# Two graph convolutions in pairs of tiles: one scan and one signal for two transposes and two products

## The chip, the cores and the metric

The kernel runs on one core of a Trainium2 chip. The core has five engines that run side by side: TensorE (PE, products and transposes), VectorE (DVE), ScalarE (ACT), GpSimd (POOL) and SyncE (SP); SP and POOL issue transfers here. Time is device microseconds of one execution, from the timed runs without the profiler; the lower the better. Engines hand work to each other by semaphores.

## The reference, cut to what matters

The model has two layers on a graph of 50000 nodes with 128 features and 25000 edges, sorted by their target. The first is an attention layer over typed edges (not touched here). The second does two graph convolutions in a row over the same edges:

```python
def _graph_conv(h, src, dst, W, b):
    n = h.shape[0]
    ones = jnp.ones(src.shape[0], dtype=h.dtype)
    out_deg = jnp.clip(jax.ops.segment_sum(ones, src, num_segments=n), 1.0)
    in_deg = jnp.clip(jax.ops.segment_sum(ones, dst, num_segments=n), 1.0)
    h = h * jax.lax.rsqrt(out_deg)[:, None]
    agg = jax.ops.segment_sum(h[src], dst, num_segments=n)
    agg = agg * jax.lax.rsqrt(in_deg)[:, None]
    return jax.nn.relu(agg @ W + b)

h = _graph_conv(features, src, dst, W1, b1)
h = _graph_conv(h, src, dst, W2, b2)
...
x = x + _L1_gnn_ref(h, ...)
```

## The kernel before, in words

The edges are cut into `ET` = 196 tiles of 128. Both convolutions are one function, `conv_phase(second)`, called twice; each walks over the 196 tiles, and each engine has its own list of instructions, written out in full.

For tile n, with edges on partitions and features in columns:

- POOL gathers the 128 source rows from memory into `row` (L1592). A ring of `R` = 14 tiles holds them; gather n waits for transpose n-14.
- In the second convolution ACT multiplies the rows by the source's factor (L1629), in place.
- PE transposes the tile into `pT` (L1644), so that edges lie along the columns.
- DVE scans along the edges (L1669): state = keep x state + value. `keep` is 0 where a new target begins and 1 elsewhere, so the state at a target's last edge is the sum over its edges. The scan starts with the last column of the tile before, so the scans form one chain through all 196 tiles. The result goes to the ring `sT`.
- PE multiplies by the weights (L1650) into `pm`; the scan's result is the stationary operand. An fp32 product is two instructions in the profile, a transpose one.
- DVE scales by the target's factor and adds the bias (L1676).
- First convolution: ACT applies the ReLU (L1632) and SP stores the tile to the table `t1` (L1619), from which the second one gathers. Second convolution: DVE applies the ReLU and adds the old x in one operation (L1681), for which SP loads the tile `rx` (L1615), and POOL scatters the rows to the output (L1598), only those of a target's last edge.

What sets the order: PE does transpose n, then product n-1; `pT` and `pm` have two buffers each, so transpose n waits for scan n-2 and product n-1 waits for the evacuation n-3. DVE does scan n, then evacuation n-2 (and, in the second, its residual). POOL does, in the second convolution, gather n, then scatter n-8 (`LAG` = 8). SP loads a piece of `keep` of 14 tiles (448 KB) at n = 0, 14, 28, ... in the first convolution, in the same queue as the stores, which stand at n-8; the second uses the same `keep`. Between the two convolutions all engines meet at a barrier, and the stores of `t1` have landed.

## Time and profile before

| | |
|---|---|
| time, 3 runs | median 3132.02 us (3129.52 to 3133.0) |
| the profiled execution | 3122.26 us, of which the span 3120.6 us |
| first convolution, first gather to the barrier | 2257 to 2555 us |
| second convolution, first gather to last scatter | 2555 to 3113 us |
| TensorE's granted clock over the span | 0.769 |

The profile is of one execution. A row of the timeline gives an instruction's start and length in microseconds, and in brackets how long its engine had been idle and what it waited for. What is named as the releaser is inferred from semaphores, and can be the name of a transfer of another stage that once used the same semaphore. For PE, the start and length are those of the issue, with a modelled end: when its result was really there shows only in who waits for it. "issue" means that the profile shows nothing that was waited for.

### The profile page before, as it was taken

To read this page: it belongs to the slowest core of one execution; us is meant where nothing else is said; L and a number is where in the kernel's file an instruction comes from. 1 tells how busy PE (TensorE), PEld (TensorE's weight loads), DVE (VectorE), ACT (ScalarE), POOL (GpSimd) and SP (SyncE) were. 2 spreads that over 40 slices of the span, in tenths; PEclk is the share of its full clock that TensorE was granted. 3 is DMA by queue.
4 is the path that set the end of the run, shared out by engine and by line. 5 is a ranking of instruction groups with operands and counts; after the bars stand their busy time and mean duration, and the time that the engine had idled before them with its cause. 6 is when DMAs were issued, how large, how long until landed. Compare 5 with 4: busy or idle time off the path is not lost. (4 is left out here: it accounts for less than half of the span.)

```text
span 3120.6 us, 48869 instructions
## 1 busy us (share of the span) xinstructions
PE 1916.5 (61%) x12706; PEld 1487.4 (48%) x12706; DVE 2069.9 (66%) x6764; ACT 1160.4 (37%) x3211; POOL 1837.1 (59%) x2417
## 2 busy tenths in 40 slices
PE   4620006889888889898886378778555553333333
PEld 1100005788888888888886245444334432222222
DVE  7975546888888788788786777777634443333333
ACT  0000005666666666666663245545412221111111
POOL 0003327777777777777774245454466657666766
PEclk9965557999999999999998689898755555555555
DMA  1016755666666666666663244444334442222221
GB/s 48 0 37 232 246 184 146 155 157 155 156 157 155 157 152 157 158 156 151 157 157 93 52 128 116 127 122 121 98 101 116 115 101 65 64 67 63 64 64 49
DMA packets 400270, 374.38 MB, mean 120 GB/s; under 512 B 60254, under 2 KB 342269, under 8 KB 397032
## 3 DMA queue, kind: packets, MB, share of 16 engines
q1 hardware_dynamic: 360856, 276.76, 33.2%
q0 software_dynamic: 31360, 64.76, 10.0%
q10 hardware_dynamic: 7806, 29.98, 2.4%
q8 instruction: 104, 1.70, 0.2%
q14 instruction: 144, 1.18, 0.1%
HBM read 227.43 MB, written 147.13 MB: 120 GB/s over the span
## 5 line engine op out<-in xcount | busy, mean ns | idle before, releaser
L814 POOL DMA_INDIRECT att_xsd<-xt,ends_i x392 | 405.0, 1033 | 179.7 <-issue 136.6
L1669 DVE TENSOR_TENSOR_SCAN conv_sT<-keep,conv_sT,conv_pT 128x128 f32<-128x128 bf16 x390 | 186.5, 478 | 485.3 <-DMA t<-conv_res 193.7
L1650 PE MATMUL conv_pm<-w,conv_sT 128*128 128x128 f32 x784 | 280.1, 460 | 358.6 <-DVE conv_res L1676 226.9
L1650 PEld LDWEIGHTS conv_pm<-w,conv_sT 128*128 128x128 f32 x784 | 196.9, 311 | 450.0 <-issue 321.2
L1008 PE MATMUL att_kvc<-att_hm,w_kv 128*128 128x128 f32 x2352 | 296.3, 276 | 0.0
L1118 DVE TENSOR_TENSOR att_kvm<-att_kvc,att_rel_in 128x1024 f32<-128x1024 f32 x196 | 239.0, 1219 | 62.5 <-PE att_kvc L1021 50.3
L1008 PEld LDWEIGHTS att_kvc<-att_hm,w_kv 128*128 128x128 f32 x2352 | 280.3, 193 | 0.0
L1354 POOL TENSOR_TENSOR edge_glm<-edge_gl,edge_mask 128x1536 f32<-128x1536 f32 (+1 forms) x56 | 153.2, 2736 | 211.9 <-PE edge_pc L1445 205.1
L952 ACT ACTIVATE att_nhb<-att_nxr 128x128 f32<-128x128 f32 x391 | 168.7, 478 | 277.3 <-DMA att_nxr<-xt 276.9
L1107 DVE TENSOR_TENSOR att_hm<-att_hT,att_mask_in_t 128x768 f32<-128x768 f32 x196 | 186.3, 951 | 114.9 <-issue 106.3
L1598 POOL DMA_INDIRECT out_dram<-conv_res,out_i x196 | 198.1, 1011 | 108.6 <-issue 101.3
L1644 PE MATMUL conv_pT<-ident,conv_row 128*128 128x128 f32 x392 | 168.7, 430 | 147.7 <-issue 117.0
L1629 ACT ACTIVATE conv_row<-conv_row,ats 128x128 f32<-128x128 f32 x196 | 78.7, 401 | 474.1 <-DMA conv_row<-t,idx 454.9
L1592 POOL DMA_INDIRECT conv_row<-ta,idx x196 | 185.5, 946 | 103.5 <-issue 40.9
L1592 POOL DMA_INDIRECT conv_row<-t,idx x196 | 191.9, 979 | 77.2 <-issue 56.1
L1021 PE MATMUL att_kvc<-tab,att_noh 9*128 9x128 bf16 x391 | 53.6, 217 | 280.7 <-DMA att_noh<-node_hot 277.4
L1059 PE MATMUL att_msgp<-att_kvm,rel_v 128*128 128x128 f32 x1568 | 224.1, 290 | 0.0
L1057 PE MATMUL att_keyp<-att_kvm,rel_k 128*128 128x128 f32 x1568 | 223.2, 289 | 0.5 <-DVE att_prod L1099 0.5
L1059 PEld LDWEIGHTS att_msgp<-att_kvm,rel_v 128*128 128x128 f32 x1568 | 208.6, 207 | 0.0
L1057 PEld LDWEIGHTS att_keyp<-att_kvm,rel_k 128*128 128x128 f32 x1568 | 205.0, 204 | 5.0 <-issue 0.7
L1076 DVE BATCH_NORM_STATS2 att_nst<-att_nx 128x6 f32<-128x128 f32 x782 | 190.3, 285 | 13.5
L931 ACT ACTIVATE msg_all<-att_msgp 128x128 f32<-128x128 f32 x196 | 54.4, 278 | 324.4 <-PE att_msgp L1059 315.6
(242 smaller groups left out, 5012.0 us busy)
## 6 DMA issues: line engine op xcount, KB each, us to landing
att_mask_in_t<-type_row SPq DMA_DIRECT2D x196, 192.0 KB
xt<-xr ACTq DMA_DIRECT2D x23, 1224.0 KB
att_nxr<-xt SPq DMA_DIRECT2D x97, 262.0 KB
att_rel_in<-rel_row SPq DMA_DIRECT2D x196, 128.0 KB
out_dram<-att_not SPq DMA_DIRECT2D x97, 256.0 KB
ta<-att_nhs SPq DMA_DIRECT2D x97, 256.0 KB
xr<-in_x_dram SPq DMA_DIRECT2D x22, 1088.0 KB
xd_rows<-att_xsd SPq DMA_DIRECT2D x196, 65.5 KB
```

Source lines behind the costliest of these rows:

```text
L814: pool.indirect_dma_start(out=xsd[:, v, k, :], out_offset=None, in_=xt, in_offset=bass.IndirectOffsetOnAxis(ap=ends_i[:, n, k:k + 1], axis ...
L952: m = nc.scalar.activation(nhb[:, u % 2, i], nxr[g % RN][:, j, 0:D], ACT.Relu, bias=nxr[g % RN][:, j, C_NA:C_NA + 1], scale=nxr[g % RN][:, ...
L1008: nc.tensor.matmul(kvc[:, e], w_kv[:, t, e], hm[:, w, 0, t], start=e == 0 and t == 0, stop=False)
L1057: nc.tensor.matmul(keyp[:, 0], rel_k[:, r], kvm[:, w, 0, r], start=r == 0, stop=r == RELS - 1)
L1059: m = nc.tensor.matmul(msgp[:, 0], rel_v[:, r], kvm[:, w, 1, r], start=r == 0, stop=r == RELS - 1)
L1076: m = dve.bn_stats(nst[:, k, i], of[:, u % 2 * 2 + i])
L1107: dve.tensor_tensor(hm[:, w], hT[:, 0:2].rearrange("p e (o d) -> p e o d", o=1).to_broadcast([P, 2, TYPES, P]), mask_in_t[:, k % RM], ALU. ...
L1118: dve.tensor_tensor(kvm[:, w], kvc[:, 0:2].rearrange("p a (o e) -> p a o e", o=1).to_broadcast([P, 2, RELS, P]), rel_in[:, v].rearrange("p ...
L1592: pool.indirect_dma_start(out=row[:, n % R, :], out_offset=None, in_=table, in_offset=bass.IndirectOffsetOnAxis(ap=idx[:, int(second), n:n ...
L1598: pool.indirect_dma_start(out=out, out_offset=bass.IndirectOffsetOnAxis(ap=out_i[:, k:k + 1], axis=0), in_=res[:, k % R, :], in_offset=Non ...
L1650: nc.tensor.matmul(pm[:, k % 2, 0:D], sT[:, k % R], w[:], start=True, stop=True).then_inc(m_ready, 1)
L1669: dve.tensor_tensor_scan(sT[:, n % R], keep[:, n * P:(n + 1) * P], pT[:, n % 2, 0:P], before, ALU.mult, ALU.add).then_inc(s_ready, 1)
```

## The change

The two convolutions work on pairs of tiles, `H` = 98 passes. The rings hold `RP` = 14 pairs instead of 14 tiles, so twice the rows. PE transposes both tiles of pair p into one buffer of `pT`, with one signal, and then does both products of pair p - `AHEAD` = p-3, with one signal. `pT` and `pm` have four buffers each. DVE scans both tiles in one instruction of 256 columns, then evacuates the two products of pair p-4 in two instructions, and in the second convolution adds the residual in one of 256 columns. ACT applies the ReLU to a pair at once; its scaling in the second convolution stays one instruction a tile, with one signal for the pair. SP stores and loads pairs; the piece of `keep` for seven pairs is loaded at p = 0, 7, 14, ..., ahead of the store of pair p-4. POOL's gathers and scatters stay one a tile; `LAG` is 16 tiles, and waits are one a pair.

```diff
@@ -1545,8 +1545,12 @@
-        R = 14
-        CHUNKS = ET // R
+        H = ET // 2
+        RP = 14
+        USES = H // RP
+        KP = 7
+        NBANK = 4
+        AHEAD = 3
         keep = sb("keep", [P, EP], BF16)
         idx = sb("idx", [P, 2, ET], I32)

@@ -1564,21 +1568,21 @@

     ls, clear = phase_sems(name + "_")

-    LAG = 8
+    LAG = 16
     table, w, b_all = (t1, w_2, b2_all) if second else (ta, w_1, b1_all)
-    row = lb("row", [P, R, D], F32)
-    sT = lb("sT", [P, R, P], F32)
-    res = lb("res", [P, R, D], F32)
-    rx = lb("rx", [P, R, D], F32) if second else None
-    pT = lp("pT", [P, 2, 512], F32)
-    pm = lp("pm", [P, 2, 512], F32)
+    row = lb("row", [P, RP, 2, D], F32)
+    sT = lb("sT", [P, RP, 2 * P], F32)
+    res = lb("res", [P, RP, 2, D], F32)
+    rx = lb("rx", [P, RP, 2, D], F32) if second else None
+    pT = lp("pT", [P, NBANK, 512], F32)
+    pm = lp("pm", [P, NBANK, 4, D], F32)
...
     with nc.Block() as block:
         @block.gpsimd
@@ -1587,98 +1591,111 @@
                 pool.wait_ge(idx_ready, 2)
             for n in range(ET + (LAG if second else 0)):
                 if n < ET:
-                    if n >= R:
-                        pool.wait_ge(t_ready, n - R + 1)
-                    pool.indirect_dma_start(out=row[:, n % R, :], out_offset=None, in_=table,
+                    p = n // 2
+                    if p >= RP and n % 2 == 0:
+                        pool.wait_ge(t_ready, p - RP + 1)
+                    pool.indirect_dma_start(out=row[:, p % RP, n % 2, :], out_offset=None, in_=table,
                                             in_offset=bass.IndirectOffsetOnAxis(ap=idx[:, int(second), n:n + 1], axis=0)
-                                            ).then_inc(got[n % R], 16)
+                                            ).then_inc(got[p % RP], 16)
                 k = n - LAG
                 if second and k >= 0:
-                    pool.wait_ge(res_ready, k + 1)
+                    q = k // 2
+                    if k % 2 == 0:
+                        pool.wait_ge(res_ready, q + 1)
                     pool.indirect_dma_start(out=out, out_offset=bass.IndirectOffsetOnAxis(ap=out_i[:, k:k + 1], axis=0),
-                                            in_=res[:, k % R, :], in_offset=None, bounds_check=N - 1,
-                                            oob_is_err=False).then_inc(stored[k % R], 16)
+                                            in_=res[:, q % RP, k % 2, :], in_offset=None, bounds_check=N - 1,
+                                            oob_is_err=False).then_inc(stored[q % RP], 16)
...
         @block.sync
         def _(sp):
-            for n in range(ET + LAG):
-                if n < ET and n % R == 0 and not second:
-                    c = n // R
-                    sp.dma_start(keep[:, c * R * P:(c + 1) * R * P],
-                                 keep_row[c * R * P:(c + 1) * R * P].partition_broadcast(P)).then_inc(keep_in[c], 16)
-                k = n - LAG
-                if k >= 0 and not second:
-                    sp.wait_ge(res_ready, k + 1)
-                    sp.dma_start(t1[k * P:(k + 1) * P], res[:, k % R]).then_inc(stored[k % R], 16)
+            for p in range(H + AHEAD + 1):
+                if p < H and p % KP == 0 and not second:
+                    c, w0 = p // KP, KP * 2 * P
+                    sp.dma_start(keep[:, c * w0:(c + 1) * w0],
+                                 keep_row[c * w0:(c + 1) * w0].partition_broadcast(P)).then_inc(keep_in[c], 16)
...
+                q = p - AHEAD - 1
+                if q >= 0 and not second:
+                    sp.wait_ge(res_ready, q + 1)
+                    sp.dma_start(t1[q * 2 * P:(q + 1) * 2 * P].rearrange("(j e) d -> e j d", e=P), res[:, q % RP]).then_inc(stored[q % RP], 16)
...
         @block.scalar
...
         @block.tensor
         def _(pe):
-            for n in range(ET + 1):
-                if n < ET:
+            for p in range(H + AHEAD):
+                if p < H:
                     if second:
-                        pe.wait_ge(scaled, n + 1)
+                        pe.wait_ge(scaled, p + 1)
                     else:
-                        pe.wait_ge(got[n % R], n // R * 16 + 16)
-                    if n >= 2:
-                        pe.wait_ge(s_ready, n - 1)
-                    nc.tensor.transpose(pT[:, n % 2, 0:P], row[:, n % R], ident[:]).then_inc(t_ready, 1)
-                k = n - 1
-                if k >= 0:
-                    pe.wait_ge(s_ready, k + 1)
-                    if k >= 2:
-                        pe.wait_ge(v_ready, k - 1)
-                    nc.tensor.matmul(pm[:, k % 2, 0:D], sT[:, k % R], w[:], start=True, stop=True).then_inc(m_ready, 1)
+                        pe.wait_ge(got[p % RP], p // RP * 32 + 32)
+                    if p >= NBANK:
+                        pe.wait_ge(s_ready, p - NBANK + 1)
+                    for j in range(2):
+                        m = nc.tensor.transpose(pT[:, p % NBANK, j * P:(j + 1) * P], row[:, p % RP, j], ident[:])
+                    m.then_inc(t_ready, 1)
+                q = p - AHEAD
+                if q >= 0:
+                    pe.wait_ge(s_ready, q + 1)
+                    if q >= NBANK:
+                        pe.wait_ge(v_ready, q - NBANK + 1)
+                    for j in range(2):
+                        m = nc.tensor.matmul(pm[:, q % NBANK, j], sT[:, q % RP, j * P:(j + 1) * P], w[:], start=True, stop=True)
+                    m.then_inc(m_ready, 1)

         @block.vector
         def _(dve):
             if not second:
                 dve.tensor_scalar(idx[:, 0], ats[:, :, 0, 2], float(EP + NP), None, ALU.min).then_inc(idx_ready, 1)
                 dve.tensor_scalar(idx[:, 1], ats[:, :, 0, 2], float(EP), None, ALU.min).then_inc(idx_ready, 1)
-            for n in range(ET + 2):
-                if n < ET:
-                    dve.wait_ge(t_ready, n + 1)
-                    if not second and n % R == 0:
-                        dve.wait_ge(keep_in[n // R], 16)
-                    if n >= R:
-                        dve.wait_ge(m_ready, n - R + 1)
-                    if n == 0:
-                        before = 0.0
+            for p in range(H + AHEAD + 1):
+                if p < H:
+                    dve.wait_ge(t_ready, p + 1)
+                    if not second and p % KP == 0:
+                        dve.wait_ge(keep_in[p // KP], 16)
+                    if p >= RP:
+                        dve.wait_ge(m_ready, p - RP + 1)
+                    if p == 0:
+                        prior = 0.0
                     else:
-                        dve.wait_ge(s_ready, n)
-                        before = sT[:, (n - 1) % R, P - 1:P]
-                    dve.tensor_tensor_scan(sT[:, n % R], keep[:, n * P:(n + 1) * P], pT[:, n % 2, 0:P], before,
+                        dve.wait_ge(s_ready, p)
+                        prior = sT[:, (p - 1) % RP, 2 * P - 1:2 * P]
+                    dve.tensor_tensor_scan(sT[:, p % RP], keep[:, p * 2 * P:(p + 1) * 2 * P], pT[:, p % NBANK, 0:2 * P], prior,
                                            ALU.mult, ALU.add).then_inc(s_ready, 1)
-                k = n - 2
-                if k >= 0:
-                    dve.wait_ge(m_ready, k + 1)
-                    if k >= R:
-                        dve.wait_ge(stored[k % R], k // R * 16)
-                    dve.scalar_tensor_tensor(res[:, k % R], pm[:, k % 2, 0:D], ats[:, k:k + 1, 1, 1], b_all[:],
-                                             ALU.mult, ALU.add).then_inc(v_ready, 1)
+                q = p - AHEAD - 1
+                if q >= 0:
+                    dve.wait_ge(m_ready, q + 1)
+                    if q >= RP:
+                        dve.wait_ge(stored[q % RP], q // RP * (32 if second else 16))
+                    for j in range(2):
+                        k = 2 * q + j
+                        m = dve.scalar_tensor_tensor(res[:, q % RP, j], pm[:, q % NBANK, j], ats[:, k:k + 1, 1, 1], b_all[:],
+                                                     ALU.mult, ALU.add)
+                    m.then_inc(v_ready, 1)
                     if second:
-                        dve.wait_ge(x_in[k % R], k // R * 16 + 16)
-                        dve.wait_ge(v_ready, k + 1)
-                        dve.scalar_tensor_tensor(res[:, k % R], res[:, k % R], 0.0, rx[:, k % R], ALU.max,
+                        dve.wait_ge(x_in[q % RP], q // RP * 16 + 16)
+                        dve.wait_ge(v_ready, q + 1)
+                        dve.scalar_tensor_tensor(res[:, q % RP], res[:, q % RP], 0.0, rx[:, q % RP], ALU.max,
                                                  ALU.add).then_inc(res_ready, 1)
     clear()
 
```

How the lists of instructions stand now. PE at the start of the first convolution, before (`conv_pT` is the transpose, `conv_pm` the product):

```order
L1644 MATMUL conv_pT<-ident,conv_row 128x128 x2
L1650 MATMUL conv_pm<-w,conv_sT 128x128
L1644 MATMUL conv_pT<-ident,conv_row 128x128
L1650 MATMUL conv_pm<-w,conv_sT 128x128
L1644 MATMUL conv_pT<-ident,conv_row 128x128
```

and after:

```order
L1655 MATMUL conv_pT<-ident,conv_row 128x128 x8
L1663 MATMUL conv_pm<-w,conv_sT 128x128 x2
L1655 MATMUL conv_pT<-ident,conv_row 128x128 x2
L1663 MATMUL conv_pm<-w,conv_sT 128x128 x2
L1655 MATMUL conv_pT<-ident,conv_row 128x128 x2
```

Eight transposes stand before the first product, where there were two, and from then on two of each alternate.

DVE at the start of the second convolution (`conv_sT` is the scan, `conv_res` the evacuation and the residual), before:

```order
L1669 SCALAR_TENSOR_TENSOR conv_sT<-keep,conv_pT 128x128
L1669 SCALAR_TENSOR_TENSOR conv_sT<-keep,conv_sT,conv_pT 128x128 x2
L1676 SCALAR_TENSOR_TENSOR conv_res<-conv_pm,ats,b_all 128x128
L1681 SCALAR_TENSOR_TENSOR conv_res<-conv_res,conv_rx 128x128
L1669 SCALAR_TENSOR_TENSOR conv_sT<-keep,conv_sT,conv_pT 128x128
```

and after:

```order
L1683 SCALAR_TENSOR_TENSOR conv_sT<-keep,conv_pT 128x256
L1683 SCALAR_TENSOR_TENSOR conv_sT<-keep,conv_sT,conv_pT 128x256 x4
L1692 SCALAR_TENSOR_TENSOR conv_res<-conv_pm,ats,b_all 128x128 x2
L1698 SCALAR_TENSOR_TENSOR conv_res<-conv_res,conv_rx 128x256
L1683 SCALAR_TENSOR_TENSOR conv_sT<-keep,conv_sT,conv_pT 128x256
```

The first result stands behind five scans of two tiles, where it stood behind three of one tile.

SP in the first convolution (the loads of `keep` and the stores), before:

```order
L1610 DMA keep<-keep_row 128x1792
L1619 DMA t<-conv_res 128x128 x6
L1610 DMA keep<-keep_row 128x1792
L1619 DMA t<-conv_res 128x128 x14
L1610 DMA keep<-keep_row 128x1792
```

and after:

```order
L1617 DMA keep<-keep_row 128x1792
L1626 DMA t<-conv_res 128x2x128 x3
L1617 DMA keep<-keep_row 128x1792
L1626 DMA t<-conv_res 128x2x128 x7
L1617 DMA keep<-keep_row 128x1792
```

The second piece, for tiles 14 and on, stood behind the store of tile 5; now it stands behind the store of pair 2, that is of tiles 4 and 5. What differs is when that store's result is made: tile 5 by DVE's pass 7, pair 2 by its pass 6, the last one before the scan of pair 7, which is tiles 14 and 15.

## Rows read from the trace of the kernel before

**Rows 1.** Stretches, both convolutions: length, busy us (instructions) of each engine, clock, DMA share, GB/s

```profile
2257.00:2555.00 298.00, 165.51 (x588) 116.97 (x588) 136.90 (x393) 60.67 (x196) 185.46 (x196) 0.52 0.40 108
2555.00:3113.00 558.00, 191.65 (x588) 120.91 (x588) 193.35 (x588) 78.66 (x196) 389.64 (x392) 0.50 0.27 65
```

**Rows 2.** Groups by line, GpSimd: count | busy us, mean ns | idle us before

```profile
L1592 POOL DMA_INDIRECT conv_row<-ta,idx x196 | 185.5, 946 | 103.5 <-issue 40.9 <-PE conv_pT L1644 35.2 <-DMA att_noh<-node_hot 18.7
L1598 POOL DMA_INDIRECT out_dram<-conv_res,out_i x196 | 198.1, 1011 | 108.6 <-issue 101.3 <-DVE conv_res L1681 7.3
L1592 POOL DMA_INDIRECT conv_row<-t,idx x196 | 191.9, 979 | 77.2 <-issue 56.1 <-POOLq L109 17.8 <-DVE conv_res L1681 1.8
```

**Rows 3.** Timeline, ends of both stages: start, length, engine, line, operation [idle before]

```profile
2257.37 1.09 POOL L1592 DMA_INDIRECT conv_row<-ta,idx  x1 [8.73 <-DVE idx L1656]
2260.25 0.48 PE L1644 MATMUL conv_pT<-ident,conv_row 128*128 128x128 f32 x1 [17.32 <-DMA conv_row<-ta,idx]
2536.65 0.94 POOL L1592 DMA_INDIRECT conv_row<-ta,idx  x1 [0.30 <-issue]
2555.36 0.94 POOL L1592 DMA_INDIRECT conv_row<-t,idx  x1 [17.76 <-POOLq L109]
```

**Rows 4.** Timeline, VectorE: first and last scan of the first convolution

```profile
2260.76 0.42 DVE L1669 TENSOR_TENSOR_SCAN conv_sT<-keep,conv_pT 128x128 f32<-128x128 bf16 x1 [3.68 <-PE conv_pT L1644]
2549.10 0.48 DVE L1669 TENSOR_TENSOR_SCAN conv_sT<-keep,conv_sT,conv_pT 128x128 f32<-128x128 bf16 x1
```

**Rows 5.** Timeline, first convolution, where tiles go quickly

```profile
2503.12 0.48 DVE L1669 TENSOR_TENSOR_SCAN conv_sT<-keep,conv_sT,conv_pT 128x128 f32<-128x128 bf16 x1 [0.54 <-PE conv_pT L1644]
2503.76 0.48 DVE L1669 TENSOR_TENSOR_SCAN conv_sT<-keep,conv_sT,conv_pT 128x128 f32<-128x128 bf16 x1
2504.55 0.42 PE L1644 MATMUL conv_pT<-ident,conv_row 128*128 128x128 f32 x1
2505.01 0.48 DVE L1669 TENSOR_TENSOR_SCAN conv_sT<-keep,conv_sT,conv_pT 128x128 f32<-128x128 bf16 x1 [0.53 <-issue]
2505.19 0.42 PE L1644 MATMUL conv_pT<-ident,conv_row 128*128 128x128 f32 x1
```

**Rows 6.** Groups by line, VectorE: a scan of 384 columns, stage before

```profile
L1489 DVE TENSOR_TENSOR_SCAN msg_all<-edge_dB,msg_all 128x384 f32<-128x384 f32 x28 | 28.5, 1017 | 26.0 <-PE edge_dB L1429 26.0
```

**Rows 7.** Timeline, first convolution, where scans come late

```profile
2270.17 0.48 PE L1644 MATMUL conv_pT<-ident,conv_row 128*128 128x128 f32 x1 [0.34 <-DMA conv_row<-ta,idx]
2271.62 0.47 PE L1644 MATMUL conv_pT<-ident,conv_row 128*128 128x128 f32 x1
2274.09 0.48 DVE L1669 TENSOR_TENSOR_SCAN conv_sT<-keep,conv_sT,conv_pT 128x128 f32<-128x128 bf16 x1 [3.53 <-DMA att_noh<-node_hot]
2278.32 0.48 DVE L1669 TENSOR_TENSOR_SCAN conv_sT<-keep,conv_sT,conv_pT 128x128 f32<-128x128 bf16 x1 [3.50 <-DMA att_noh<-node_hot]
2293.72 0.48 DVE L1669 TENSOR_TENSOR_SCAN conv_sT<-keep,conv_sT,conv_pT 128x128 f32<-128x128 bf16 x1 [3.48 <-DMA att_noh<-node_hot]
```

**Rows 8.** Timeline of SyncE's queue, a load of `keep`; then stretches behind it

```profile
2303.35 0.43 SPq L1610 DMA_DIRECT2D keep<-keep_row  x1
...
2307.40:2308.40 1.00, 0.00 (x0) 0.00 (x0) 0.00 (x0) 0.00 (x0) 0.00 (x0) 0.50 0.48 129
2308.40:2309.40 1.00, 0.00 (x0) 0.00 (x0) 0.09 (x1) 0.00 (x0) 0.00 (x0) 0.50 0.03 8
```

**Rows 9.** Timeline, second convolution: a gather, its result, its scatter

```profile
2889.29 0.98 POOL L1592 DMA_INDIRECT conv_row<-t,idx  x1 [0.30 <-issue]
2899.50 0.29 DVE L1681 SCALAR_TENSOR_TENSOR conv_res<-conv_res,conv_rx 128x128 f32<-128x128 f32 x1
2911.37 1.01 POOL L1598 DMA_INDIRECT out_dram<-conv_res,out_i  x1 [0.30 <-issue]
```

**Rows 10.** Timeline, GpSimd, second convolution: first and last scatter that waited

```profile
2580.56 1.01 POOL L1598 DMA_INDIRECT out_dram<-conv_res,out_i  x1 [1.26 <-issue]
3094.22 1.01 POOL L1598 DMA_INDIRECT out_dram<-conv_res,out_i  x1 [2.65 <-issue]
```

37 lines of the change are left out of this document (20 added, 17 removed).

## The prediction

> **What bounds the kernel now.** I read the busy time by stage first. The change touches two stages alone: the first convolution, about 2257 to 2555 us, and the second, 2555 to 3113 us. In both TensorE's granted clock is about 0.50, the lower of its two levels, and no engine's busy time fills the stage [rows 1]. What lies ahead of 2257 us is left as it is.
>
> Then the groups by line. In the second convolution GpSimd issues 196 gathers and 196 scatters: 191.9 + 198.1 us busy, and before them 77.2 + 108.6 us idle, of which 17.8 us are the change of stage. GpSimd's own pace is one issue after another with 0.30 us between them [rows 9], so its floor is 191.9 + 198.1 + 391 x 0.30 = 507.3 us, and it took 390.0 + 168.0 = 558.0 us [rows 2]: 50.7 us above its floor. In the first convolution it issues gathers alone: floor 185.5 + 196 x 0.30 = 244.3 us, taken from 2257.37 to 2537.6, which is 280 us; the next stage's first gather starts at 2555.36 [rows 2, 3]. So the first convolution is not bound by GpSimd: the rows are there, and TensorE and VectorE are late. Their scans run from 2260.76 to 2549.10 us, 288.3 us for 195 steps, 1.479 us a tile [rows 4].
>
> Then the timeline, for what a tile costs TensorE and VectorE. There are two regimes. In the quick one, two tiles take 2503.12 to 2505.01 = 1.89 us, 0.945 a tile, though the engines alone could do better: two scans with the other VectorE operation between them lie 0.64 us apart, and two transposes with a product between them also 0.64 us (2504.55 to 2505.19) [rows 5]. The 0.3 us more is the round trip: a product waits for the scan just before it, and that scan for a transpose that stands behind the product before. In the slow one, a transpose starts at 2270.17 and the scan that reads it only at 2274.09; the next at 2271.62, its scan at 2278.32 [rows 7]. VectorE had nothing else to do; the name behind its idle time is a DMA of another stage, which it does not wait for. So what is late is TensorE's completion, by 3 to 6 us. Four steps on, a scan starts at 2293.72: 19.6 us from the first, 4.9 a tile. I don't know what causes it. What I can count is its cost: 288 us less 195 x 0.945 = 184 us is 104 us in the first convolution, 7.4 us for 14 tiles.
>
> **The change, part by part.**
>
> *Signals and order.* TensorE does two transposes, then the two products of the pair three back; nothing in a pass waits for a scan of the same pass. The round trip goes, and what is late next is TensorE itself at 0.64 us a tile, 1.28 a pair. VectorE: a 128-wide scan and one evacuation cost 0.64; a scan of 256 columns I put between the 0.48 of 128 and the 1.017 of 384 columns [rows 5, 6], 0.75 us, so a pair is 0.64 + 0.27 + 0.33 = 1.24 us, no more than TensorE. Bounds: the scan costs 0.48 at the least and 1.02 at the most, the pair 0.97 to 1.51. In the second convolution the residual over 256 columns adds at most 2 x 0.29, and GpSimd takes 5.2 us a pair, so nothing of this shows there.
>
> *The slow regime* is left: the number of transposes and products is the same. I keep 7.4 us for 14 tiles. It could go down to 0, if fewer waits of TensorE make it rarer, or stay in full.
>
> *The table `keep`.* This edit speaks against the change. SyncE loads a piece of 448 KB every 14 tiles and stands in its own queue behind the store of a result. Before, the store ahead of it is that of tile n-9, and the load has some seven tiles of time. After, it is the store of pair p-5, whose result VectorE makes in the last pass before the one that needs the piece. So each of 13 loads is waited for: the ReLU, 0.4 us, the issue of the store and the load, 0.7 us, and the transfer. Traffic after the load issued at 2303.35 dies away by 2308.4 [rows 8], with other traffic in it; the smallest transfer shown, a gather to its transpose, takes 2257.37 to 2260.25 = 2.9 us [rows 3]. Between 2.9 and 5.0 I take 4.0, nearer the load's own row; the wait is 5.1 us. Behind it on VectorE stand all later scans and evacuations. TensorE has three pairs in hand, 3 x 1.28 = 3.8 us, so it loses 5.1 - 3.8 + the scan's 0.75 = 2.0 us every 14 tiles.
>
> *First convolution, the sum.* Per 14 tiles: 14 x 0.64 = 9.0, slow regime 7.4, `keep` 2.0, together 18.4 us, against GpSimd's 14 x 1.25 = 17.5. So TensorE's side still sets it, by a little: 14 x 18.4 = 258 us from a first scan at 2260.8 + 1.25 (a pair needs two gathers), that is to 2520; before, 6.3 us lie between the last scan's start and the next stage's first gather, and I add 0.5 for the longer tail: 2526 against 2555.4, a gain of 29 us. The best is GpSimd's floor: last gather 2257.4 + 195 x 1.25 = 2501.1, + 2.9 to its transpose, + 0.6 to the scan, + 6.8 = 2511.4, a gain of 44. The worst, with nothing hidden, is in the rivals.
>
> *Second convolution, the sum.* GpSimd waits only where a result is late for its scatter. Before, the gather at 2889.29 has its result at 2899.79, and its scatter starts at 2911.37: 11.6 us of reserve [rows 9]. The scatters that wait longer than 0.4 us are 27, in 13 clusters, the first at 2580.56 and the last at 3094.22 [rows 10]; these are the slow regime, when results slip past the reserve. After, a scatter stands 16 gathers back instead of 8, at 16 x 2.60 + 1.3 = 42.9 us behind its gather. But its result waits for the scan of four pairs on, nine gathers later: 9 x 2.60 = 23.4, then the 5.3 us that also remain before (10.5 less two periods), and 1.35 for a second scaling (0.40), transpose (0.21), the wider scan (0.27), a second evacuation (0.33) and the wider residual (0.14): 30.0. Reserve 12.9, or 1.3 us more for 13 clusters: 17 us. Doubling the distance buys so little because the deeper pipeline spends it. I take 22, near that end; the bounds are 0 and the whole 50.
>
> *Everything else*: half as many stores, of 128 KB, off the path; one ReLU instead of two, hidden behind GpSimd's 1.25 us a tile; start and end of the second stage keep their single gathers and scatters. Nothing.
>
> *A rule that could speak against it.* In the second convolution TensorE now works in bursts, one in 5.2 us instead of 2.6, and the clock there is already at its lower level, 0.50 [rows 1]. The Trainium skill, "TensorE: Matmul & The Clock Gate", section "Loop structure matters more than you think", says that waits between bursts of products send the engine back to its cold clock. By the trace this costs 0, since there is nothing to lose; by the rule, had the stage run at 2.4 GHz, a tile's 0.64 would have been half and would now double, still under the 2.60 of GpSimd.
>
> Total: 29 + 22 = 51 us. The profiled execution took 3122.3 us, so 3071; the median of the runs shown is 3132.0, 9.8 above it, and I carry that over: 3081 us.
>
> **Rivals.**
>
> B, the late completions lose their bite: with three pairs of slack both stages run at GpSimd's floor. 44 + 50 us: 3122.3 - 94 + 9.8 = 3038. For it: the slow regime is a matter of lateness, and slack absorbs lateness. Against it: in it TensorE serves a tile in 4.9 us and one arrives in 1.25, and slack does not add service.
>
> C, the load of `keep` is paid in full in the first convolution, because it and the slow regime fall apart in time and the three pairs in hand are mostly done when the wait starts. Per 14 tiles 9.0 + 7.4 + 5.1 = 21.5 us, 301 in all against 288: 13 us lost, 22 won in the second: 3123.
>
> D, slower: C, and the round trip does not go, because the wide scan sits at its upper bound and every pair is handed on in lumps. Then 14 x 0.945 + 7.4 + 5.1 = 25.7 us, 360 in all: 72 lost, 22 won, 3182. It decides as soon as 14 tiles of the first convolution cost more than 20.7 + 22/14 = 22.3 us. For it: both new dependences sit in that stage. Against it: nothing in a pass waits for the same pass any more.
>
> E: the change does not reach the path, the slow regime fills whatever is freed: 3132.
>
> **How the numbers follow.** My forecast 0.56, B 0.17, C 0.14, D 0.08, E 0.05. The predicted time is 3081. The range runs to the times of B and C, 3040 to 3125, and leaves out about 0.2. A measurement of this kernel tells 0.2%, 6 us, from no change. Faster: forecast, B and half of C (which ends 9 us below the median, at the edge of what counts), 0.80; same: E and 0.03 of C, 0.08; slower: D and the last 0.04 of C, 0.12.
>
> **What would show it.** Right: between slow stretches transposes of a pair and products of a pair follow each other at 1.28 us a pair or at GpSimd's 2.5; scans of 256 columns near 0.75 us; every seventh scan of the first convolution waits 3 to 5 us behind the load of `keep`; the next stage's first gather near 2526; in the second convolution fewer scatters wait, and the slow stretches are still there. Wrong: slow stretches gone or shorter (B), 14 tiles of the first convolution above 20.7 us (C, D), scans above 1 us, or a second convolution still 50 us above GpSimd's floor.

## The result, and the profile after

The changed kernel takes 3154.05 us (median of 4 runs, 3152.42 to 3156.05) against 3132.51 for the kernel before beside it (4 runs, 3129.52 to 3136.21): ratio 1.0069, 95% interval 1.0058 to 1.0081. It is slower by 21.5 us; I had forecast 51 us faster, and the time lies outside my range.

The two convolutions in the view of stretches, from each one's first gather (columns as in [rows 1], which these answer to; the second reaches to the end of the execution here):

```profile
2258.95:2572.85 313.90, 125.19 (x588) 109.38 (x588) 117.23 (x294) 40.84 (x98) 185.06 (x197) 0.60 0.37 103
2572.85:3153.10 580.25, 153.47 (x588) 120.27 (x588) 162.11 (x392) 67.90 (x196) 390.16 (x392) 0.51 0.26 62
```

The work got cheaper as planned: VectorE's busy time in the first falls from 136.9 to 117.2 us. The stage got longer all the same, 313.9 us for 298.0, although TensorE's granted clock rose in it from 0.52 to 0.60. The groups by line say that the instructions cost what I took, and that GpSimd waits more for results (busy, mean ns | idle before, releasers; the GpSimd rows answer to [rows 2]):

```profile
L1683 DVE TENSOR_TENSOR_SCAN conv_sT<-keep,conv_sT,conv_pT 128x256 f32<-128x256 bf16 x194 | 144.2, 744 | 562.4 <-DMA t<-conv_res 213.7 <-PE conv_pT L1655 167.5 <-issue 90.9
L1605 POOL DMA_INDIRECT out_dram<-conv_res,out_i x196 | 197.9, 1010 | 120.0 <-issue 66.3 <-DVE conv_res L1698 53.7
L1597 POOL DMA_INDIRECT conv_row<-t,idx x196 | 192.3, 981 | 91.6 <-issue 58.5 <-POOLq L109 32.3 <-DMA t<-conv_res 0.9
```

A scan of 256 columns takes 744 ns. The scatters' idle time is 120.0 us, before 108.6; the gathers' is the same once the wait between the stages is taken off (91.6 - 32.3 against 77.2 - 17.8).

The ends of the stages on the timeline, as in [rows 3]:

```profile
2258.95 1.09 POOL L1597 DMA_INDIRECT conv_row<-ta,idx  x1 [8.73 <-DVE idx L1670]
2539.63 0.94 POOL L1597 DMA_INDIRECT conv_row<-ta,idx  x1 [0.30 <-issue]
2572.85 0.94 POOL L1597 DMA_INDIRECT conv_row<-t,idx  x1 [32.27 <-POOLq L109]
3141.35 0.98 POOL L1605 DMA_INDIRECT out_dram<-conv_res,out_i  x1 [0.30 <-issue]
```

The two profiled executions (spans 3153.1 and 3120.6) lie 32.5 us apart, and the medians only 21.5: the profiled one of the kernel before is 10 us quicker than its median. The parts below are those of this one pair, so the sizes of the middle two are uncertain by some 10 us. The 32.5 us divide into:

| part | us |
|---|---|
| first convolution starts later | 1.6 |
| its first gather to the next stage's: 313.9 for 298.0 | 15.9 |
| GpSimd waits longer for results in the second | 11.4 |
| last scatter's start to the end: 11.8 for 8.2 | 3.6 |

A second profiled execution of the changed kernel (after_again, below) has 310.0 us in the first convolution and 571.1 from there to the end, where the kernel before has 298.0 and 565.2: 12.0 and 5.9 us lost, 3.6 of the latter at the end. That the second convolution won nothing is thus seen twice; the 11.4 us is not (2.3 there).

The 15.9 us divide again, by the times of the scans. The first 13 pairs take 68.2 us where the first 26 tiles took 51.1: 17.1 lost. The rest takes 233.0 where it took 237.3: 4.2 won. The first scan comes 1.25 us later behind the first gather, and the stage ends 1.8 us later behind the last scan. So most of the loss is one place, the first stretch of late completions:

```profile
2276.49 0.75 DVE L1683 TENSOR_TENSOR_SCAN conv_sT<-keep,conv_sT,conv_pT 128x256 f32<-128x256 bf16 x1 [1.57 <-issue]
2289.88 0.75 DVE L1683 TENSOR_TENSOR_SCAN conv_sT<-keep,conv_sT,conv_pT 128x256 f32<-128x256 bf16 x1 [12.14 <-DMA att_noh<-node_hot]
2306.06 0.75 DVE L1683 TENSOR_TENSOR_SCAN conv_sT<-keep,conv_sT,conv_pT 128x256 f32<-128x256 bf16 x1 [14.94 <-DMA att_noh<-node_hot]
2319.36 0.75 DVE L1683 TENSOR_TENSOR_SCAN conv_sT<-keep,conv_sT,conv_pT 128x256 f32<-128x256 bf16 x1 [12.05 <-DMA att_noh<-node_hot]
```

The scans come 13.4, 16.2 and 13.3 us apart. The releaser named, a DMA of an earlier stage, is only the nearest event of the record; in the trace's semaphore events each of the last three scans starts 0.03 us behind TensorE's signal that the pair is transposed (2289.85, 2306.03, 2319.33), and that signal is what is late. This is the slow regime of [rows 7]; in the kernel before a tile took up to 6.3 us there, and a pair takes up to 16.2 now.

After that the stage goes in cycles of seven pairs, most of them 20 to 21 us long and 19.4 on average (233.0 us for 84 pairs). The last gap of a cycle is the wait for `keep`:

```profile
2436.46 0.75 DVE L1683 TENSOR_TENSOR_SCAN conv_sT<-keep,conv_sT,conv_pT 128x256 f32<-128x256 bf16 x1 [5.16 <-DMA att_noh<-node_hot]
...
2438.59 0.47 SPq L1617 DMA_DIRECT2D keep<-keep_row  x1
2438.63 0.44 PEld L1655 LDWEIGHTS conv_pT<-ident,conv_row 128*128 128x128 f32 x2
2438.84 0.64 PE L1655 MATMUL conv_pT<-ident,conv_row 128*128 128x128 f32 x2
...
2443.53 0.75 DVE L1683 TENSOR_TENSOR_SCAN conv_sT<-keep,conv_sT,conv_pT 128x256 f32<-128x256 bf16 x1 [5.83 <-issue]
...
2444.90 0.93 PEld L1663 LDWEIGHTS conv_pm<-w,conv_sT 128*128 128x128 f32 x4 [5.83 <-issue]
2444.93 1.19 PE L1663 MATMUL conv_pm<-w,conv_sT 128*128 128x128 f32 x4 [5.46 <-DVE conv_res L1692]
```

The load is issued behind the result of the pair before it, 2.1 us after that pair's scan, and the scan starts 4.9 us later, 7.1 us behind the one before instead of 1.2. Over the twelve loads behind the first stretch the gap is 4.8 to 5.9 us longer than 1.2, on average 5.4. TensorE's last transposes end at 2439.5; then it idles for over 5 us.

### The profile page after: what moved, and what is told of

Same layout as the page of the kernel before. It is cut to its first block and busy times, and to the rows that moved or that the text cites. A ratio compares the mean times of both kernels' runs of the same rounds, so it can differ in the third digit from the quotient of the medians.

```text
span 3153.1 us, 47390 instructions
## 1 busy us (share of the span) xinstructions
PE 1835.9 (58%) x12706; PEld 1475.2 (47%) x12706; DVE 2020.3 (64%) x6470; ACT 1129.0 (36%) x3113; POOL 1836.0 (58%) x2417
## 5 line engine op out<-in xcount | busy, mean ns | idle before, releaser
L1683 DVE TENSOR_TENSOR_SCAN conv_sT<-keep,conv_sT,conv_pT 128x256 f32<-128x256 bf16 x194 | 144.2, 744 | 562.4 <-DMA t<-conv_res 213.7
L1655 PE MATMUL conv_pT<-ident,conv_row 128*128 128x128 f32 x392 | 122.2, 412 | 401.8 <-issue 249.2
L1663 PE MATMUL conv_pm<-w,conv_sT 128*128 128x128 f32 x784 | 201.2, 408 | 199.1 <-DVE conv_res L1692 128.0
L1663 PEld LDWEIGHTS conv_pm<-w,conv_sT 128*128 128x128 f32 x784 | 176.7, 311 | 216.3 <-DVE conv_sT L1683 111.6
L1655 PEld LDWEIGHTS conv_pT<-ident,conv_row 128*128 128x128 f32 x392 | 65.3, 204 | 433.9 <-issue 270.0
L1597 POOL DMA_INDIRECT conv_row<-t,idx x196 | 192.3, 981 | 91.6 <-issue 58.5
L1638 ACT ACTIVATE conv_row<-conv_row,ats 128x128 f32<-128x128 f32 x196 | 67.9, 393 | 483.7 <-DMA conv_row<-t,idx 467.0
```

The source lines that it names most:

```text
L1597: pool.indirect_dma_start(out=row[:, p % RP, n % 2, :], out_offset=None, in_=table, in_offset=bass.IndirectOffsetOnAxis(ap=idx[:, int(seco ...
L1655: m = nc.tensor.transpose(pT[:, p % NBANK, j * P:(j + 1) * P], row[:, p % RP, j], ident[:])
L1663: m = nc.tensor.matmul(pm[:, q % NBANK, j], sT[:, q % RP, j * P:(j + 1) * P], w[:], start=True, stop=True)
```

## Experiments

My theory after the result: two steps of the sum failed, the wait for `keep` (5.4 us for 2.0 in a cycle) and the reserve of the second convolution. The rival: the late completions have no fixed price, and take back whatever slack is given.

The runs fell on four chips, and these differ. The kernel before takes 3124.4 and 3131.5 us in two sessions on one of them, like the 3132.5 of the first result (its chip isn't known), and 3027.6, 3028.0 and 3027.1 on the three others. Nearly all of the 100 us lies in the two convolutions: b_lag12, on one of the three, has 254.5 and 515.1 us there against 298.0 and 565.2, 93.6 of the 96.7 us between the two spans, and its trace shows no late stretch of TensorE's signals. Ratios are to the kernel before on the same chip and in the same session; I call these *late* and *punctual* chips, though only the late one was used in more than one session.

The late traces differ in one more way. They lack records of semaphore events, of all engines, and most where the completions are late. In the first convolution of the kernel before, 279 of TensorE's 392 signals are recorded and 97 signals of VectorE's 196 scans; in b_lag12 on the punctual chip, nearly all. The same kernel compared stage by stage:

| stretch | semaphore events, b_lag12_2 (late) | b_lag12 (punctual) | TensorE's signals in the late one |
|---|---|---|---|
| 1000 to 1300 us | 5647 | 7080 | up to 1.3 us late |
| 2000 to 2240 us | 1820 | 1780 | in time |
| 2600 to 3000 us, second convolution | 1225 | 8177 | many us late |

The traces hold equally many instructions, 48869. So the recording of events and the late signals go together, and a rival is that the recording itself holds TensorE up on that chip. No run settles it: the times are said above to be those of runs without the profiler, but every timed run of the experiments has a span and a granted clock on record, so none is known to have run with nothing recording.

| run | edit | chip | us | ratio, 95% interval |
|---|---|---|---|---|
| a_keep | `keep` 7 pairs earlier | punctual | 3033.3 | 1.0020, 1.0011 to 1.0030 |
| a_keep_lag24 | + scatters 24 tiles behind | punctual | 3033.4 | 1.0017, 1.0008 to 1.0027 |
| b_lag12 | before, scatters 12 behind | punctual | 3028.0 | 1.0005, 0.9996 to 1.0015 |
| b_fill | before, wide filler | punctual | 3027.4 | 1.0001, 0.9991 to 1.0010 |
| after_again | the changed kernel | late | 3141.2 | 1.0054, 1.0038 to 1.0071 |
| a_keep_2 | as a_keep | late | 3134.1 | 1.0029, 1.0016 to 1.0041 |
| a_keep_lag24_2 | as a_keep_lag24 | late | 3128.4 | 1.0013, 1.0003 to 1.0022 |
| b_lag12_2 | as b_lag12 | late | 3124.7 | 0.9999, 0.9989 to 1.0008 |
| b_fill_2 | as b_fill | late | 3155.5 | 1.0069, 1.0053 to 1.0086 |
| b_fill_tiny | before, narrow filler | late | 3152.7 | 1.0068, 1.0051 to 1.0085 |
| b_onepass | before, one product pass (weights left out) | late | 3115.2 | 0.9942, 0.9925 to 0.9958 |
| a_keep_fill | a_keep + wide filler, 3 buffers for 4 | late | 3165.9 | 1.0109, 1.0092 to 1.0126 |
| b_allbf16 | before, all bf16 | punctual | 3027.3 | 1.0000, 0.9990 to 1.0010 |
| a_allbf16 | a_keep, all bf16 | punctual | 3030.4 | 1.0010, 1.0000 to 1.0019 |
| b_plain | before, plain row loads (permutation left out) | punctual | 2979.7 | 0.9845, 0.9829 to 0.9862 |
| b_bf16w | before, products bf16 | punctual | 3026.5 | 0.9998, 0.9989 to 1.0008 |
| b_allbf16_2 | as b_allbf16 | punctual | 3026.7 | 0.9998, 0.9989 to 1.0008 |
| b_plain_2 | as b_plain | punctual | 2979.8 | 0.9845, 0.9829 to 0.9862 |

### The wait for keep: a_keep, after_again, a_keep_2

```diff
-if p < H and p % KP == 0 and not second:
-    c, w0 = p // KP, KP * 2 * P
-    sp.dma_start(keep[...piece c...])
+if p < H and p % KP == 0 and not second:
+    for c in ((0, 1) if p == 0 else (p // KP + 1,)):
+        if c < H // KP: sp.dma_start(keep[...piece c...])
```

> The changed kernel, with each piece of keep loaded seven pairs earlier (two pieces at the start). Theory 1, the load of keep is waited for in full: the changed kernel's first convolution goes in a fixed cycle of 20.3 us for 14 tiles, of which 5.6 us are the late piece. Without it 14.7 us are left, under GpSimd's 17.5, so the stage falls to about 260 us from 313 and the kernel to about 3100, 0.990 of before. Rival, the slow regime sets the cycle and only fills other waits: the stage stays at 300 us or more and the kernel at 3140 or more.

> The changed kernel itself, beside the kernel before. Two cases. If the kernel before takes about 3132 us here (late TensorE completions present): this one 3154 again, the first gather of the second convolution 314 us after that of the first, seven scans per 20.3 us. If the kernel before takes about 3028 us (none present): my theory says that the late load of keep costs nothing at all there, since seven pairs take TensorE and VectorE 6 x 1.28 + 6.8 = 14.5 us and GpSimd's gathers of them 14 x 1.249 = 17.5 us: the gathers stay 1.25 us apart, and the time is that of the version with keep loaded seven pairs earlier, 3033 (ratio 1.002), 3.6 us of which are GpSimd's drain at the end of the second convolution (7.6 us instead of 4.0). Rival: the wait for keep is paid there too, 13 x 5 = 65 us, 3095.

> The changed kernel with each piece of keep loaded seven pairs earlier (two at the start). With late completions present: my theory is that 5.6 of the 20.3 us of seven pairs in the first convolution are the wait for keep. Without it the seven take 14.7 us and GpSimd's own 17.5 us bound them: 13 x 2.8 = 36 us less than the changed kernel, 3118, with the second convolution unchanged (568 us). Rival (the late completions follow the scans whatever these wait for, the wait only covers them): 20 us per seven pairs stay, 3154. Without late completions: 3033, as before.

On the late chip the early load gives 7 us, where my theory said 36 and the rival none. The wait is gone, some 65 us in twelve loads, and the first convolution falls only from 310.0 us in after_again to 301.4: the late completions fill most of the place. The scans of a_keep_2 in one cycle, with the same columns as above:

```profile
2437.45 0.75 DVE L1685 TENSOR_TENSOR_SCAN conv_sT<-keep,conv_sT,conv_pT 128x256 f32<-128x256 bf16 x1 [6.45 <-DMA att_noh<-node_hot]
2438.62 0.74 DVE L1685 TENSOR_TENSOR_SCAN conv_sT<-keep,conv_sT,conv_pT 128x256 f32<-128x256 bf16 x1
...
2443.23 0.74 DVE L1685 TENSOR_TENSOR_SCAN conv_sT<-keep,conv_sT,conv_pT 128x256 f32<-128x256 bf16 x1
2444.81 0.75 DVE L1685 TENSOR_TENSOR_SCAN conv_sT<-keep,conv_sT,conv_pT 128x256 f32<-128x256 bf16 x1 [0.34 <-PE conv_pT L1657]
2453.24 0.75 DVE L1685 TENSOR_TENSOR_SCAN conv_sT<-keep,conv_sT,conv_pT 128x256 f32<-128x256 bf16 x1 [7.18 <-DMA att_noh<-node_hot]
2460.24 0.75 DVE L1685 TENSOR_TENSOR_SCAN conv_sT<-keep,conv_sT,conv_pT 128x256 f32<-128x256 bf16 x1 [5.76 <-DMA att_noh<-node_hot]
```

More pairs go quickly now (1.2 us apart), but the two late ones come 8.4 and 7.0 us apart; this cycle, 2437.45 to 2460.24, holds eight pairs in 22.8 us. Over everything behind the first 13 pairs a tile takes 1.34 us here (224.5 us for 84 pairs), 1.39 in the changed kernel (233.0) and 1.40 in the one before (237.3 us for 169 tiles). On the punctual chip the gathers of a_keep stand 1.25 us apart throughout and no slack is needed; what is left of the change costs 6 us, 3.6 of them the end of the last stage. No run shows the late load of `keep` on a punctual chip.

Both convolutions on the punctual chip, first of b_lag12 (near enough the kernel before) and then of a_keep:

```profile
2254.27:2508.78 254.51, 176.79 (x588) 122.46 (x588) 138.56 (x392) 60.60 (x196) 185.07 (x197) 0.50 0.46 127
2508.78:3023.90 515.12, 178.05 (x588) 119.85 (x588) 198.72 (x588) 78.65 (x196) 388.86 (x392) 0.50 0.30 70
```

```profile
2252.94:2509.02 256.08, 141.77 (x588) 117.43 (x588) 122.35 (x294) 40.79 (x98) 185.08 (x197) 0.55 0.46 126
2509.02:3028.90 519.88, 149.65 (x588) 121.08 (x588) 164.05 (x392) 67.91 (x196) 389.99 (x392) 0.50 0.30 69
```

In both kernels both stages stand at GpSimd's floor (244 and 507 us by the prediction's sums from [rows 2], plus filling and draining). The change saves TensorE, VectorE and ScalarE 28, 35 and 11 us of work in the second convolution, and none of it is on the path.

### More reserve: b_lag12, b_lag12_2, a_keep_lag24, a_keep_lag24_2

```diff
-                LAG = 8
+                LAG = 12
```

(in the changed kernel with the early load, 16 becomes 24)

> The kernel before, with the scatter 12 gathers behind instead of 8 and nothing else. Reserve 11.6 + 10.4 = 22 us against a delay of 15: theory 1 says that nearly no scatter waits, the second stage falls from 557 to 508 us and the kernel to about 3083, 0.984. Rival (something else holds GpSimd): 3132.

> The kernel before with each scatter of the second convolution 12 tiles behind its gather instead of 8. With late completions present: the reserve grows from 11.6 to 16.8 us, over the 15.4 us that the tiles fall behind in a stretch, so the 13 clusters of stalls of 4 us go: 3132 - 50 = 3082. Rival (average pace, not reserve, is the bound): 3125 or more. Without late completions: 3028, no change.

> As a_keep, and the scatter of the second convolution stands 24 gathers behind instead of 16. Theory 1 for the second stage, the deeper pipeline used up the reserve (13 us, while a slow stretch delays a result by 19): with 34 us of reserve no scatter waits, the stage falls from 568 us to GpSimd's 507, and the kernel to about 3040, 0.970 of before. Rival, GpSimd is held by something else than late results: the second stage stays above 550, the kernel near 3100.

> The same, and in the second convolution each scatter follows its gather by 24 tiles instead of 16. With late completions present: GpSimd's reserve grows from 13 to some 23 us (8 x 1.3 more), over the 18.8 us by which the pairs fall behind in a stretch; the some 12 stalls of 5.5 us go: 3118 - 60 = 3058. Rival (the pairs fall behind by whatever the reserve allows, since TensorE and VectorE are slower on average than GpSimd): under 20 us gained, 3100 or more. Without late completions: 3033.

My reserve theory falls: 4 tiles more give nothing (0.9999), 8 more give 5.7 us where it said 60. The room given is larger than the expectations of b_lag12_2 and a_keep_lag24_2 say: a tile of distance is a gather and a scatter, 2.6 us and not 1.3. Where nothing is late, a scatter starts 11.6 us behind its result in the kernel before [rows 9] and 22.0 us (median) in b_lag12, 13.2 us in a_keep and 34.0 in a_keep_lag24. So 10 us more of room bought nothing, and 21 us more bought 5.7. The pace over many tiles is what binds, and lateness grows into the room it gets. Scans of b_lag12_2 in the second convolution, the last quick one and those behind it:

```profile
2830.70 0.47 DVE L1669 TENSOR_TENSOR_SCAN conv_sT<-keep,conv_sT,conv_pT 128x128 f32<-128x128 bf16 x1
2834.24 0.48 DVE L1669 TENSOR_TENSOR_SCAN conv_sT<-keep,conv_sT,conv_pT 128x128 f32<-128x128 bf16 x1 [2.42 <-DMA t<-conv_res]
2839.16 0.48 DVE L1669 TENSOR_TENSOR_SCAN conv_sT<-keep,conv_sT,conv_pT 128x128 f32<-128x128 bf16 x1 [3.80 <-DMA t<-conv_res]
...
2853.89 0.48 DVE L1669 TENSOR_TENSOR_SCAN conv_sT<-keep,conv_sT,conv_pT 128x128 f32<-128x128 bf16 x1 [4.50 <-DMA t<-conv_res]
2860.90 0.48 DVE L1669 TENSOR_TENSOR_SCAN conv_sT<-keep,conv_sT,conv_pT 128x128 f32<-128x128 bf16 x1 [5.89 <-DMA t<-conv_res]
2867.23 0.48 DVE L1669 TENSOR_TENSOR_SCAN conv_sT<-keep,conv_sT,conv_pT 128x128 f32<-128x128 bf16 x1 [5.20 <-DMA t<-conv_res]
2868.27 0.47 DVE L1669 TENSOR_TENSOR_SCAN conv_sT<-keep,conv_sT,conv_pT 128x128 f32<-128x128 bf16 x1
```

The gaps grow from 3.5 to 7.0 us and then drop to 1.04. Late stretches (over 2 us in which a TensorE signal comes over 0.15 us behind its instruction's end, from those semaphore events that are recorded) hold some 60% of the second convolution in the kernel before and some 80% here and in a_keep_lag24_2.

### Work or instructions: b_fill, b_fill_2, b_fill_tiny, a_keep_fill

```diff
 nc.tensor.matmul(pm[:, k % 2, 0:D], sT[:, k % R], w[:], ...).then_inc(m_ready, 1)
+for _ in range(3 if second else 1):
+    nc.tensor.matmul(spare[:], identb[:], keep[:, 0:512], start=True, stop=True)   # tiny: 0:8
```

(TensorE also waits for the first piece of `keep` before it starts; a_keep_fill has two and six fillers a pair, and three buffers of `pT` and `pm` instead of four)

> The kernel before, where TensorE does products that nobody reads behind each product: one of 512 columns a tile in the first convolution, three in the second, in bf16. Theory A, the late completions come with a TensorE that is mostly idle (in the attention stage, where it is busy, they are short): they vanish or shrink, scans wait less in both stages, and the kernel goes to 3040 to 3100. Theory B, they come with the number of its instructions or with time: more instructions make them as frequent or more so, 3132 to 3250.

> The kernel before with filler on TensorE in both convolutions: after each tile one (first) or three (second) bf16 products of 512 columns into a bank that nobody reads. It computes the same. Where late TensorE completions are present (the kernel before at 3124 to 3132): if a TensorE with long idle gaps delivers its completions late, the filler closes the gaps and the stretches vanish as they do in the attention stage: first convolution 254 us, second 515, some 3028 in all (ratio 0.969). If instead each TensorE instruction's completion costs time (a limit on completions), 2 more instructions beside the present 6 per tile in the first and 6 more in the second make it slower: 3200 or more. If neither: 3125. Where they are absent (3028): 3028 again.

> The same instructions, each filler product only 8 columns wide: as many TensorE instructions as in the wide filler, hardly any work. Late completions present: idle theory 3110 to 3130 (gaps stay), limit on completions 3200 or more. Absent: 3028.

> The changed kernel with keep loaded seven pairs earlier, three banks in place of four, and per pair two (first convolution) or six (second) filler products of 512 columns. Late completions present: idle theory, no stretches are left and GpSimd's floor bounds both convolutions: 3033 (ratio 0.97), no better than the same filler in the kernel before, since both stand at GpSimd's floor and this one has 3.6 us more drain at the end. Limit on completions: 3200 or more. Absent: 3033.

On the late chip both fillers cost, and as much whether wide or narrow: 24.0 and 21.2 us. More work on TensorE does not make the late stretches go. That its idle gaps cause them is not refuted by this, because the filler stands behind the product, which itself waits for a scan, so the long gaps stay. Two transposes of b_fill_2 and the products behind them:

```profile
2704.02 0.42 PE L1647 MATMUL conv_pT<-ident,conv_row 128*128 128x128 f32 x1
2708.57 0.77 PE L1653 MATMUL conv_pm<-w,conv_sT 128*128 128x128 f32 x2 [4.12 <-DVE conv_sT L1674]
...
2710.41 0.42 PE L1647 MATMUL conv_pT<-ident,conv_row 128*128 128x128 f32 x1 [0.22 <-issue]
2715.71 0.77 PE L1653 MATMUL conv_pm<-w,conv_sT 128*128 128x128 f32 x2 [4.88 <-DVE conv_res L1681]
```

In the second convolution TensorE idles for over 2 us at a time for 238 us in all with the wide filler, and for 202 us in the kernel before. Idle gaps alone are not enough, though: on the punctual chips TensorE has as little to do and nothing is late. First convolution of b_fill_2, then of b_fill_tiny:

```profile
2253.87:2557.92 304.05, 187.31 (x769) 120.30 (x785) 138.18 (x392) 60.59 (x196) 185.06 (x197) 0.75 0.39 106
```

```profile
2256.35:2562.96 306.61, 186.00 (x785) 142.48 (x785) 139.43 (x392) 60.69 (x196) 185.51 (x196) 0.50 0.38 106
```

The granted clock is 0.75 in the one and 0.50 in the other, the stages 304 and 307 us: the clock does not matter here. On the punctual chip the same wide filler is free (1.0001), so it is not its own time that costs on the late one. The limit on completions has the right sign; its 3200 or more was far too high.

### Fewer or cheaper passes: b_onepass, b_bf16w, b_allbf16, b_allbf16_2, a_allbf16

```diff
-sT = lb("sT", [P, R, P], F32)
+sT = lb("sT", [P, R, P], BF16)
-nc.tensor.matmul(pm[:, k % 2, 0:D], sT[:, k % R], w[:], ...)
+nc.tensor.matmul(pm[:, k % 2, 0:D], sT[:, k % R], identb[:], ...)   # b_bf16w: weights cast to bf16
```

(b_allbf16: the transposes too, as bf16 products of the upper halves of the fp32 words)

> The kernel before with the scans of the convolutions written in bf16 and multiplied by the bf16 identity in place of the weights: one product pass per tile instead of two, so 4 TensorE instructions per tile instead of 6 (the convolutions' weights are left out of the result). Late completions present: with a limit on completions, a tile in a late stretch takes 7.0 x 4/6 = 4.7 us, the lateness stays within the reserve of 11.6 us, and the time falls to some 3050; idle theory: 3125 or more. Absent: 3028.

> The kernel before with only the products in bf16 (scans written in bf16, weights cast), transposes in fp32. Late completions present: as with one product pass, 3115 (0.994) by the instruction theory; fp32 theory: two of three passes are gone, below 3080. Absent: 3028.

> The kernel before with both TensorE steps of the convolutions in bf16: rows go in as the upper halves of their fp32 words, the scans are written in bf16 and the weights are cast (the result is that of bf16 inputs). As many instructions per tile as with one product pass (4). Late completions present: if they belong to fp32 passes, none are left and the time is 3028; if to instructions of any kind, it is that of one product pass, 3115 (ratio 0.994). Absent: 3028.

> The same for the changed kernel with keep loaded seven pairs earlier: 8 TensorE instructions per pair instead of 12. Late completions present: fp32 theory 3033; instruction theory 16 to 20 us under its own 3134, some 3116. Absent: 3033.

> Both TensorE steps of the convolutions of the kernel before in bf16, 4 instructions per tile instead of 6. Late completions present (the kernel before at 3124 to 3132): fp32 theory, none are left, 3028 (ratio 0.967); instruction theory, 3115 (0.994). Absent: as before, 3028 and ratio 1.000.

The fp32 product is two weight loads and two products in the trace, the bf16 one is one of each. Without the second pass the time is 3115.2 us, 16.3 less than before: the sign of the instruction theory, at a fifth of the size it said (some 3050). The stretches stay, with smaller gaps. From b_onepass, second convolution:

```profile
2639.76 0.48 DVE L1669 TENSOR_TENSOR_SCAN conv_sT<-keep,conv_sT,conv_pT 128x128 bf16<-128x128 bf16 x1 [3.79 <-DMA t<-conv_res]
2645.37 0.48 DVE L1669 TENSOR_TENSOR_SCAN conv_sT<-keep,conv_sT,conv_pT 128x128 bf16<-128x128 bf16 x1 [4.48 <-DMA t<-conv_res]
2650.96 0.48 DVE L1669 TENSOR_TENSOR_SCAN conv_sT<-keep,conv_sT,conv_pT 128x128 bf16<-128x128 bf16 x1 [4.44 <-DMA t<-conv_res]
```

5.6 us is the largest steady gap here with 4 TensorE instructions (weight loads and products) per tile, 7.7 in the kernel before with 6, and 16.1 to 16.8 for a pair with 12. All are close to multiples of 0.70 us: 8, 11, 23 and 24. In the timed runs 784 instructions fewer (2 for each of 392 tiles) gave 16.3 us and some 1570 more (2 and 6 a tile) cost 24.0 and 21.2: 21, 15 and 14 ns each. The four bf16 runs all fell on punctual chips, where there is nothing to see, so the fp32 theory was not tested by them. The late traces themselves speak against it, and against a limit on instructions alone. The stage just before the convolutions, in the kernel before (columns as in [rows 1]), and its largest group:

```profile
2000.00:2240.00 240.00, 185.22 (x946) 112.52 (x944) 186.19 (x627) 121.23 (x316) 117.00 (x57) 0.90 0.43 118
```

```profile
L1445 PE MATMUL edge_pc<-w_a,edge_glm 128*128 128x128 f32 x588 | 73.8, 282 | 0.0
```

It has 588 fp32 products of the same shape and 3.9 products a us in all, where the first convolution has 2.0; all its 108 signals are recorded, each within 0.02 us. What differs is the number of signals, 0.45 a us against 1.3. But the change halves the signals of the convolutions and leaves the late stretches, so that count alone does not settle it either.

### Without the gathers: b_plain, b_plain_2

```diff
+sp.dma_start(row[:, n % R], ta[n * P:(n + 1) * P]).then_inc(got[n % R], 16)   # first convolution, SyncE
-pool.indirect_dma_start(out=row[:, n % R, :], ...)                             # left to the second
```

> The kernel before, but in the first convolution the rows come in file order by plain loads of SyncE's queue instead of GpSimd's gathers (the gather's permutation is left out of the result); the second convolution as it is. GpSimd's floor is gone there, so with completions on time the tiles run at the quick 0.945 us: first convolution 196 x 0.95 = 186 us instead of 298. Late completions present: if they need the gathers beside them, 186 us and the whole 3132 - 112 = 3020; if TensorE's instructions alone set them off, 1.43 us per tile stay, 3132. Absent: 3028 - 60 = 2965.

> Rows of the first convolution by plain loads in file order instead of GpSimd's gathers (the permutation is left out). Late completions present: if they need the gathers beside them, the first convolution falls from 298 to some 206 us as on the other chip and the whole to 3132 - 92 = 3040; if TensorE's instructions alone set them off, it keeps 1.43 us per tile, 3130. Absent: 2980 (ratio 0.984).

Punctual both times: 48 us less, not the 60 first expected; the scans are 1.01 us apart on average (2258.47 to 2455.76), not 0.945. It confirms that GpSimd's gathers bound that stage there, and TensorE's side is next. Whether late completions need the gathers beside them stays open.

## Why the prediction was wrong

*The sizes of the instructions* were right: a scan takes 744 ns for an estimated 0.75 us; a cycle of seven pairs has four intervals of 1.2 us, where two tiles took 1.89; the round trip is gone. The granted clock in the second convolution went from 0.50 to 0.51, so TensorE's coarser bursts cost no clock there. The Trainium skill, "TensorE: Matmul & The Clock Gate", "Loop structure matters more than you think", says that waits between products keep the engine cold; the trace agrees, with 0.51 in a stage of bursts and waits.

*The slow regime, "I keep 7.4 us for 14 tiles": this step failed, and it is most of the miss.* I carried the late completions over as a fixed toll of time, spread evenly. From the first scan to the last I had put 258 us, and it took 301.2. Of these 43 us, 34 lie in the first 13 pairs, which took 68.2 us where 13/7 x 18.4 = 34.2 were forecast, and 12 in the other 84 (233.0 for 220.8); my sum had one interval too many, 2.6 us. The 2 us left of the 45 between the 29 forecast as won and the 15.9 lost are mainly the end of the stage. Three results speak against a fixed toll: with the wait for `keep` taken away the late completions took back most of it (a_keep_2), with more reserve the stretches lengthened (b_lag12_2, a_keep_lag24_2), and they cost more with more TensorE instructions and less with fewer (fillers, b_onepass). This is the mechanism of rival E, the slow regime fills whatever is freed, to which I gave 0.05; only that it would end at no change was wrong.

*`keep` at 2.0 us a cycle: failed too*, 5.4 by the trace, near rival C's 5.1. A later cycle of 19.4 us is 8.4 of quick pairs, 5.4 of `keep` and 5.6 of late completions, for 9.0, 2.0 and 7.4 in my sum. "TensorE has three pairs in hand" was wrong, since it had already handed them over when the wait began: slack counts only if it is still unspent where the wait stands. VectorE, which waits, needs the full 1.2 us for each pair behind it and can't catch up. But taking the wait away altogether was worth 7 us, not 12 x 5.4 = 65, because of the step above. Rival C named the mechanism, and its 301 us for the stage's scans is the measured number; that is in part luck, for it had 21.5 us in every cycle, where the later ones took 19.4 and the first 13 pairs 68.2. It too had 22 won in the second convolution, where nothing was.

*The second convolution, 22 us won: failed.* The reserve is as computed (12.9; a_keep has 13.2 on the punctual chip). It did not matter, since reserve is not what binds: b_lag12_2 has 10 us more and gains nothing. That pairs are worse than tiles in this stage is not shown: on the late chip a_keep_2 and a_keep_lag24_2 are 9.7 and 4.0 us slower than the kernel before in all, and 3.6 of that is the end.

*"Everything else: nothing"*: the end costs 3.6 us. Between the last scatter and the end GpSimd drains for 7.57 us in place of 3.98, in every version of the changed kernel, on both kinds of chip and with 16 or 24 scatters at the end; b_lag12 has 3.98. What in it does so was not found. On a punctual chip that is most of the 5.6 us by which a_keep is slower.

On a punctual chip my forecast would have failed more simply: the slow regime is not there (my 104 us of it were in part GpSimd's floor: the stage is 43.5 us shorter there), both stages stand at the floor of GpSimd, and nothing can be won beside it. I had taken for a property of the kernel what belongs to the chip or to what records it. No version that I ran beats the kernel before on both kinds of chip; b_onepass, which leaves the weights out, is the only one faster on the late one, and its proper form b_bf16w (1.00 on a punctual one) was not run there.

## What to carry to other kernels

Before an edit is priced against a stall, ask whether the stall is a fixed time or a pace: add slack alone (here a distance of 12 for 8) and see whether it pays. Slack ahead of an engine covers a wait only in so far as it has not been handed over when the wait starts. Where the rest above the bounding engine's floor is a stall of unknown cause, time the kernel on more than one chip before it is tuned for that stall, and compare how many events the traces hold stage by stage: a trace that lacks them where the stall stands may be part of the stall. Filler behind an instruction that waits doesn't fill the wait.
